# Score banks, one bank for turned weights, and a fused way out of PSUM in the first attention of a four-layer kernel

## What is computed

```python
x = x + L0_xattn(layernorm(x), ctx, ctx)   # 16 heads of width 8, softmax over 77 context rows
x = x + L0_ffn(layernorm(x))               # 8 experts, 2 chosen for each row, SiLU-gated
x = x + L1_xattn(layernorm(x), ctx)        # attention with softmaxed features, no score matrix
x = x + L1_ffn(layernorm(x))               # 8 experts, 2 chosen, and 2 shared ones, GELU
```

```python
score = einsum('bhqd,bhkd->bhqk', q, k) / sqrt(8)
attn  = softmax(score, axis=-1)            # 128 queries x 16 heads x 77 keys in each tile
out   = einsum('bhqk,bhkd->bhqd', attn, v) @ Wo.T + bo
```

## Time and profile before

| | us |
|---|---|
| median of 3 runs | 783.42 (781.82 to 787.84) |
| the profiled execution | 779.32 |
| its span in the profile | 777.3 |
| PE busy in the span | 685.8 (88%) |
| DVE busy | 465.3 (60%) |
| POOL busy | 382.0 (49%) |
| ACT busy | 326.5 (42%) |

### The profile page before, as it was taken

The page is one execution under the profiler, slowest core; times in us unless marked ns, Lnnn a source line. Parts: engine busy times, 40 slices in busy tenths (PEclk is TensorE's granted clock), DMA queues, the critical chain, the costliest instruction groups (busy, mean ns, idle before and its releaser), DMA issues.

```text
span 777.3 us, 15729 instructions
## 1 busy us (share of the span) xinstructions
PE 685.8 (88%) x5140; PEld 505.9 (65%) x5140; DVE 465.3 (60%) x1348; ACT 326.5 (42%) x689; POOL 382.0 (49%) x502
## 2 busy tenths in 40 slices
PE   7989999999898968899878799999999689999990
PEld 3556666667666668788776445555544289999990
DVE  4556877787677667776547766667553423333326
ACT  3434455445333232222212466666764244444440
POOL 5213176566537624556561365555555425545552
PEclk9999999999889789999987899999999999999995
DMA  6811111221101567777663000000000578877669
GB/s 165 251 22 9 10 32 22 31 30 25 33 10 36 127 175 235 236 227 234 196 212 91 1 24 22 21 29 25 21 29 29 131 247 266 262 245 237 220 200 283
DMA packets 102119, 91.34 MB, mean 118 GB/s; under 512 B 52952, under 2 KB 85848, under 8 KB 101720
## 3 DMA queue, kind: packets, MB, share of 16 engines
q1 hardware_dynamic: 86375, 68.80, 32.5%
q0 software_dynamic: 8640, 17.84, 6.5%
q10 hardware_dynamic: 7025, 3.70, 1.8%
HBM read 69.13 MB, written 22.72 MB: 118 GB/s over the span
## 4 chain that ended last, share of the span: by engine, by line
PE 50%; DVE 18%; SPq 10%; issue 9%; POOL 4%; ACT 4%; DMA 4%; another core or an unknown queue 2%; POOLq 0%; DVEq 0%
PE pair L1356 26%; PE pair L1662 9%; PE pair L1359 7%; DVE sm L1119 3%; SPq L417 2%; POOL xs_sorted L554 2%; DVE smax L1115 2%; PE pair L1714 2%; PE pair L1462 2%; DMA xr<-xs_sorted 2%; ACT xa L664 2%; PE pair L1477 2%; SPq L431 1%; PE pair L1397 1%
## 5 line engine op out<-in xcount | busy, mean ns | idle before, releaser
L627 POOL DMA_INDIRECT y_tok<-ysb,xr x142 | 137.6, 969 | 141.0 <-DVE ysb L1035 104.4
L554 POOL DMA_INDIRECT xs_sorted<-xa,slot_i x128 | 130.6, 1020 | 92.8 <-DVE slot_i L942 58.3
L1356 PE MATMUL pair<-xT,w_all 128*128 128x256 f32 (+1 forms) x640 | 140.5, 364 | 0.0
L1356 PEld LDWEIGHTS pair<-xT,w_all 128*128 128x128 f32 x640 | 110.4, 197 | 10.0
L1662 PEld LDWEIGHTS pair<-w_all,hT 128*128 128x128 f32 x852 | 106.2, 192 | 7.6 <-issue 4.4
L1662 PE MATMUL pair<-w_all,hT 128*128 128x128 f32 x852 | 108.3, 275 | 3.0 <-DVE hT L1022 2.2
L1014 DVE COPY xT<-pair 128x256 f32<-128x256 f32 (+1 forms) x80 | 31.5, 393 | 107.1 <-PE pair L1359 80.9
L804 ACT ACTIVATE hT<-pair,w_all 128x256 f32<-128x256 f32 (+1 forms) x160 | 61.5, 449 | 79.0 <-PE pair L1356 78.5
L1115 DVE TENSOR_REDUCE smax<-pair 128x8 f32<-128x616 f32 x64 | 50.4, 787 | 31.4 <-PE pair L1356 31.1
L1356 PE MATMUL pair<-xeT_all,w_sh 128*128 128x512 f32 x128 | 69.0, 622 | 0.0
L800 ACT ACTIVATE hg<-pair,w_all 128x256 f32<-128x256 f32 (+1 forms) x80 | 31.7, 447 | 88.1 <-PE pair L1356 59.2
(11 more groups left out here) (197 smaller groups left out, 1125.1 us busy)
## 6 DMA issues: line engine op xcount, KB each, us to landing
w_all<-in_w SPq DMA_DIRECT2D x40, 578.0 KB
w_all<-in_w SPq DMA_DIRECT2D x40, 450.0 KB
xa<-y_tok SPq DMA_DIRECT2D x32, 256.0 KB, 4.2
xr<-xs_sorted SPq DMA_DIRECT2D x62, 130.0 KB
y_tok<-ysb,xr POOLq DMA_INDIRECT x142
xs_sorted<-xa,slot_i POOLq DMA_INDIRECT x128
out<-x_sb ACTq DMA_DIRECT2D x8, 256.0 KB, 3.3
xs_sorted<-in_pads SPq DMA_DIRECT2D x12, 130.0 KB, 3.9
```

The lines of the kernel that those rows point to most:

```text
L554: g.indirect_dma_start(xs_dram[l], bass.IndirectOffsetOnAxis(ap=slot_i[:, i:i + 1], axis=0), xa[:, GT * c + j // TOPK, j % TOPK, :], None) ...
L627: g.indirect_dma_start(y_dram[l], bass.IndirectOffsetOnAxis(ap=xr[u % NXR][:, t, P:P + 1].bitcast(I32), axis=0), ysb[u % NYB][:, t, :], None)\
L1356: return mm(out_, l_, r_, start=True, stop=True)
```

## The change

Six edits, all in the first attention:

1. The two halves of the scores get their own banks (0, 1 and 2, 3), and a half's score waits for the subtraction of the same half of the tile before. PE now computes both halves of tile T+1 during tile T.
2. All turned groups go to bank 4, one at a time: each turn waits for the exponential of the turn before it. The turns are spread out singly, with other PE work between them.
3. Numerators of two tiles and their sums share bank 5 (columns 0 to 383). After every second tile ACT copies them to SBUF (`raw`), a new copy of 384 columns (`sums_and_values`); DVE adds the two sums (a new operation) and takes the reciprocal.
4. The ACT copy of the expanded reciprocals (`rdx`) goes; DVE reads them from PSUM in `output`.
5. On ACT, the four pieces of `keep_input` and of `norm_input` are spread between the exponentials.
6. On SP's queue, `values(1)` to `values(3)` stand ahead of the padding rows and of a few small loads.

```diff
@@ SP
             inputs(NEARLY * GT, NT, f"x_in{NEARLY}")
+            values(1)
             row(2, "bq1", "bias_in1")
...
+            values(2)
             sp.dma_start(w_sh[:], a["ws"]).then_inc(S("ws_in"), 16)
+            values(3)
             for l in range(2):
...
-            for u in range(1, NGRP):
+            for u in range(4, NGRP):
                 values(u)
@@ ACT
-                def expanded(u):
-                    act.wait_ge(S("rdx_done"), u + 1)
-                    copy_out(rdx[:], bank[rdx_bank(u)][:]).then_inc(S("rdx_ready"), 1)
+                def sums_and_values(T):
+                    u, t = divmod(T, GT)
+                    act.wait_ge(S("pvd_done"), T + 1)
+                    after(act, S("o_ready0"), u)
+                    copy_out(raw[:, t // 2, :], bank[5][:, 0:3 * P]).then_inc(S("raw_kept"), 1)
...
+                        exps(T, (0,))
+                    pieces(0, 1)
+                    if live(v):
+                        exps(T, (1,))
+                    if s == 0 and live(v - 1):
+                        sums_and_values(T - 1)
+                    pieces(1, 3)
                     if s == 2 and live(v + 1):
                         input_turned(v + 1)
                     if live(v):
-                        exps(T, (2, 3))
+                        exps(T, (2,))
+                    pieces(3, 4)
+                    if s == 2 and live(v):
+                        sums_and_values(T - 1)
+                    if live(v):
+                        exps(T, (3,))
@@ DVE
                 def inverse_sums(u):
-                    dve.wait_ge(S("pvd_done"), GT * (u + 1))
-                    v.reciprocal(rden[:], bank[5][:, 0:P]).then_inc(S("rden"), 1)
+                    dve.wait_ge(S("raw_kept"), GT // 2 * (u + 1))
+                    after(dve, S("rdx_done"), u)
+                    link(v.tensor_tensor(rden[:], raw[:, 0, 2 * P:3 * P], raw[:, 1, 2 * P:3 * P], ALU.add))
+                    v.reciprocal(rden[:], rden[:]).then_inc(S("rden"), 1)
...
                 def output(u):
-                    dve.wait_ge(S("rdx_ready"), u + 1)
-                    dve.wait_ge(S("pvn_done"), GT * (u + 1))
-                    v.tensor_tensor(oT0, bank[4][:], rdx[:], ALU.mult).then_inc(S("o_ready0"), 1)
+                    dve.wait_ge(S("rdx_done"), u + 1)
+                    v.tensor_tensor(oT0.rearrange("p (k c) -> p k c", k=2), raw[:, :, 0:2 * P],
+                                    bank[rdx_bank(u)][:].rearrange("p (k c) -> p k c", k=2), ALU.mult).then_inc(S("o_ready0"), 1)
...
-                inverse_sums(U_LAST)
                 gates(0, U_LAST - 2)
                 slots(0, U_LAST - 2)
+                inverse_sums(U_LAST)
@@ PE
-                    after(pe, S("s_sub"), 2 * T + ab)
+                    after(pe, S("s_sub"), 2 * T + ab - 1)
...
-                        after(pe, S("exp_done"), G - 1)
+                        after(pe, S("exp_done"), G)
...
+                    if 0 <= T + 1 < NT:
+                        score(T + 1, 0)
                     if live(v):
-                        score(T, 1)
+                        turns(T, (0,))
+                    if T in (0, 1):
+                        busy(1, 4, 6)
+                    if T > 0:
+                        weighted(T - 1)
                     if s == 1 and live(v - 2):
                         logits(v - 2)
                     if live(v):
-                        turns(T, (0, 1))
...
+                        turns(T, (1,))
+                    if T > 0 and s == 0:
+                        summed(T - 1)
                     if s == 1 and live(v - 1):
                         expand(v - 1)
...
                     if 0 <= T + 1 < NT:
-                        score(T + 1, 0)
+                        score(T + 1, 1)
                     if live(v):
-                        turns(T, (2, 3))
+                        turns(T, (2,))
...
                     if T > 0 and s > 0:
                         summed(T - 1)
+                    if s == 0 and live(v + 1):
+                        keys(v + 1)
+                    if live(v):
+                        turns(T, (3,))
                     if s == 0 and live(v - 2):
                         kept_turned(v - 2)
```

More of the change, by code:

```diff
@@ L703, in exps @@
                         n = unit_columns(gr)
[L704 removed]
+                        s_.activation(pT[T % 2][gr][:, 0:n], bank[4][:, 0:n], ACT.Exp, scale=SCALE)\
                             .then_inc(S("exp_done"), 1)
@@ L1439, in turns @@
                         pe.wait_ge(S("s_sub"), 2 * T + gr // 2 + 1)
-                        after(pe, S("exp_done"), G - 1)
+                        after(pe, S("exp_done"), G)
                         for i in range(unit_columns(gr) // P):
-                            last = turn(tile(bank[2 + gr % 2], i), tile(sm[gr // 2], 3 * (gr % 2) + i))
+                            last = turn(tile(bank[4], i), tile(sm[gr // 2], 3 * (gr % 2) + i))
                         last.then_inc(S("t_done"), 1)
@@ L1461, in weighted @@
                             at = (gr * 3 + i) * 32
-                            last = mm(tile(bank[4], t)[r, :], vm(u, t)[:, at:at + 32], weights_of(T, gr, i),
-                                      start=(i == 0), stop=(i == 2))
+                            last = mm(tile(bank[5], t % 2)[r, :], vm(u, t)[:, at:at + 32], weights_of(T, gr, i),
+                                      start=(t % 2 == 0 and i == 0), stop=False)
                     last.then_inc(S("pvn_done"), 1)
@@ L1476, in summed @@
                             at = (t * 6 + gr % 2 * 3 + i) * 32
-                            last = mm(bank[5][r, 0:P], dcst[:, at:at + 32], weights_of(T, gr, i),
-                                      start=(t == 0 and i == 0), stop=(t == GT - 1 and i == 2))
+                            last = mm(tile(bank[5], 2)[r, :], dcst[:, at:at + 32], weights_of(T, gr, i),
+                                      start=False, stop=(t % 2 == 1 and i == 2))
                     last.then_inc(S("pvd_done"), 1)
```

51 lines of the change are left out of this document (19 added, 32 removed).

## The result

| | us |
|---|---|
| kernel after, median of 4 runs | 813.89 (808.89 to 824.38) |
| kernel before, median of 4 runs | 782.62 (780.46 to 787.84) |
| ratio, 95% interval | 1.0374 (1.0318 to 1.0430) |
| the profiled execution of after, its span | 815.29, 813.3 |

The ratio leaves out one execution of the kernel after (824.38 us), which lies over 1.5% above its fastest, at a lower clock. The change made the kernel 31 us slower: 813.9 us, where 782 was said and 766 to 792 was the range. First the page of the kernel after: busy times, and the clock that PE was granted in 40 slices of 20.3 us.

A forecast was written before the change was run, and what follows sets the result against it. PE was taken as nearest to the bound, DVE second, each waiting for the other. Start -3.2, five groups +6.1, tiles 29 to 31 -2.5, end +1.4: +1.8 us on 779.3, 781.1, stated as 782 us, range 766 to 792.

The forecast's parts named there:

- 5 x 27.83 = 139.15 then: Tile 9 to tile 29: five groups at the forecast period of 27.83 us, against 133.0 now, +6.1 us.
- rival 2: PE's stand at s = 1 brings its clock down in every group, 5 x 2.8 = 14 us, 795 us; chance 0.17.
- The maxima lost their waits: DVE's maxima no longer wait for scores, save at the first tile; 0.45 + 0.97 us a group can go.
- The logits' wait: DVE's copy of the logits at s = 1 waits 3.11 us a group instead of 2.55.
- that ahead of the addition: DVE waits 0.87 us a group for the sums, now copied through ACT, ahead of the new addition.
- The turn with one bank: At s = 0 PE may stand about 0.5 us between the last two turns; counted as nothing.
- 5 groups 133.0 us now: Baseline from tile 9 to tile 29 in the kernel before, 206.66 - 73.65 = 133.0 us.
- Column sums, 1.17 us: DVE waits 1.17 us a group at the column sums in s = 3, where it waited for a score before.
- -2.5 us: Tile 29 to 31 takes 15.6 us instead of 18.11 if the slow stretch does not come again.
- The sentence that six groups of short gaps run at 1.00: Argument on the clock: the kernel before keeps full clock through six groups of short PE gaps, tile 29 excepted.
- SP's queue, -4.6: values(1) lands earlier, so PE's 3.33 us wait at tile 4 and the slow blocks behind it go, -4.6 us.
- The end, +1.4: Between the last sums and the last expansion PE waits 1.8 us against 0.42, +1.4 us.

The follow-up runs named there:

- quiet set: A set of runs taken together on one chip in which the kernel before takes about 748 us; in disturbed sets it takes about 783.
- f3: Kernel before with the 40 scatters of groups 0 to 4 moved from POOL's loop to behind it; tile 9 to 29 took 134.3 us.
- f4: Kernel after with the next group's first score moved behind the column sums; ratio to before 1.0130, tile 9 to 29 in 136.7 us.
- g4: Kernel after with POOL's eight scatters a group issued one by one between its other instructions; ratio to before 1.0252.
- g2: Kernel after, unchanged, run where the kernel before takes 748 us; ratio to before 1.0244, tile 9 to 29 in 141.5 us.
- f2: Kernel after with the 40 scatters of groups 0 to 4 moved behind POOL's loop; tile 9 to 29 took 141.5 us (before takes 750).
- h1: Kernel after with the first context keys computed ahead of the last expansion; ratio to before 1.0205, tile 9 to 29 in 141.5 us.
- h4: The kernel of f2 once more, kernel after with 40 scatters behind the loop; tile 9 to 29 took 141.5 us (before takes 748).
- i2: Kernel after with the 40 scatters moved behind POOL's loop, where before takes 785 us; tile 9 to 29 took 141.5 us.
- f1: Kernel before with only values(1) to values(3) put ahead of the padding DMAs on SP; ratio to before 0.9986.
- g1: Kernel before, unchanged, run where it takes 748 us; tile 9 to 29 took 131.2 us.
- h3: Kernel after with first score later, logits later and context keys ahead of the last expansion; ratio to before 1.0022, tile 9 to 29 in 128.8 us.
- j1: The kernel of h3 once more, in another set; ratio to before 1.0026, tile 9 to 29 in 128.7 us.
- i4: Kernel before, unchanged, run again for its trace where it takes 785 us; tile 9 to 29 took 134.3 us.
- i1: Kernel after, unchanged, run again where the kernel before takes 785 us; tile 9 to 29 took 157.9 us.

## Why the prediction was wrong

**The step that failed** is the one that carries the loop, "5 x 27.83 = 139.15 then". It measured 159.4 us. Its terms were nearly right for PE and DVE when no signal is late (141.5). What the sum had at nothing is that PE's signals arrive late beside POOL's scatters, and that PE then runs at half speed behind the stands: 17.9 of the 20 us. The range had no room for it: its top, 792, was half of rival 2.

**Right.** The maxima lost their waits. The logits' wait was 3.14 us where no signal was late (3.11 said), that ahead of the addition 0.84 (0.87 said), the addition 0.29 us (0.25), the wait ahead of the last expansion 1.93 to 2.11 (1.8). The turn with one bank stood 0.34 us at s = 0, and nowhere else in a clean group (0.5 said). A clean group took 28.3 us, 27.8 were said.

**The baseline (the step "5 groups 133.0 us now").** I took that as the kernel's own pace. Between the first maxima of tiles 9 and 29 the same trace has 133.9, and quiet sets have 131.2 and 131.3. By these marks the forecast is +5.3 (139.15 less 133.86) and a quiet set has +10.3 (141.5 less 131.2): 2.7 of the 5 us between them are the baseline and 2.3 the clean group. The trace of before held late signals and one fall of the clock in its loop; f3, without late signals, takes 134.3, so the 2.7 us are not shown to be theirs alone.

**Column sums, 1.17 us.** It was 1.83. The step summed PE's work from the subtraction of s = 2 and left out that the first score of s = 3 waits for `qT_ready`; my own order rows had that wait in them. PE stands 0.78 us there in each group. f4 shows the price with and without: 1.55 us a group, since the sums also lie behind that score. The clean group is 0.49 over the forecast: 0.66 here and 0.2 ahead of the addition of the projection, which no step had, less some 0.4 by which DVE's own work was put too high.

**Late signals.** This is the larger part in the first result: 159.4 - 141.5 = 17.9 us of the loop. No step had it. The rows were there: the earlier trace rows shows PE standing 1.29 us ahead of the logits of tile 29, and the ACT copy that it waits for was itself waiting for a signal of PE that was 1.7 us late. I counted that stand as a loss that the change would not meet again (-2.5 us), and never asked what had made it. In the changed order the waits for the logits, the projection and the sums through ACT all start with a signal of PE near POOL's pairs of scatters.

**Rival 2, the clock.** It named a real loss and priced its cause wrongly. By its own sign it was met: 8 of the 34 windows of 5 us from 60 to 230 show a clock under 0.9, where more than two were asked. But it was to come from the gap of about 0.5 us at s = 1 by itself, in every group. That gap is 0.45 us in a clean group, and by itself it brought the clock down in two groups of f4 and one of g4, for 1.4 us each and not 2.8, and in none of g2, f2, h1, h4 or i2. In the kernel after it was the late signals that made stands of 1.3 to 2.3 us. The sentence that six groups of short gaps run at 1.00 was wrong too: the window of the kernel before from 180 to 210 us shows 0.92. By the Trainium skill (TensorE: Matmul & The Clock Gate, "A second HAM failure mode: psum-queue depth-cycling") short stands between groups of matmuls are enough to make the clock go back and forth. The trace of f4 agrees (0.94 from 60 to 90 and from 150 to 180 us, behind a stand of 0.45); those of g2 and i2, with the same stands at 1.00, show that it does not always happen.

**SP's queue, -4.6.** The tile 4 stand went, but f1 says that the whole gives 1.1 us, with 0 inside the interval. The step took a wait of one execution for a property of the kernel.

**The end, +1.4.** PE's wait grew as said; what it costs was mis-sized, because three pieces behind it run at half speed. From the last maximum to the last scatter g2 takes 3.7 us more than g1, and with the stand filled 3.1 (h3), 1.7 (j1) or none (h1) of it go, by the clock behind.

Sum for a quiet set: 10.3 us in the loop, 0.6 in tiles 29 to 31 and 3.7 in the tail, less 1.3 that the start brought (tile 9 at 69.87 against 71.16), 13.3 us, and the spans of g1 and g2 (750.9 and 764.2) differ by just that. The ratio makes it 18; g1's one execution, 752.9, lies 5 above the median of its kernel. For the first result: 24.7 us at the last expansion (231.21 to 255.90) and 36 between the spans. Of the 11 behind it, 7.3 lie behind the first routed turn (500.6 and 507.9 us from there to the end), in code that the change does not touch; in the second pair, i4 and i1, the spans differ by 26.0, and from that turn on they take the same (505.7 and 505.9). So these 7 us belong to the two executions and not to the change, and the cause is open.

## What to carry over

When work moves from one place of a queue to another, list every semaphore that it waits for at its new place, and what else must be done by then. A wait that is far from binding at the old place (here the queries) binds at the new one. A period read from one trace is the kernel's own only if its waits are explained: a signal that arrives 1 us or more after the work is done comes from outside the program's order, and its price moves with the order. And a forecast from one execution should be asked what would be different in another; here the same two kernels differ by 2.4% in one set and by 3.7% in the other.

## What was unexpected of the hardware

PE's semaphore signals can be held back while GpSimd issues indirect DMAs. They then come together, 0.3 to 1.7 us behind the end of a scatter (mostly about 0.6), 0.3 to 3 us late; PE's own work goes on. No matched signal of DVE (229) or ACT (125) is late in the kernel after; of those 17 and 12 that left no record, 22 were followed within 0.12 us by an instruction that waits on their semaphore. It happens at some times and not at others with the same program: 22 to 27 of 219 to 246 matched signals from 60 to 232 us in the five traces with scatters in the loop where the kernel before takes 783 us, none of 252 in the one without them there (i2), and at most 2 of about 255 in the fourteen traces where it takes 748. One chip number stands on both sides, so a chip by itself does not explain it. By the Trainium skill (SBUF — State Buffer, "SBUF: two separate sides") PE never waits for another engine at SBUF; the trace agrees as far as PE's instructions go, and shows that its signals are another matter.
